# Inverse roots of a fused attention, local-attention and expert kernel: exp(-0.5 ln) on ScalarE in place of Sqrt, reciprocals and two of three Newton steps

## What is computed

```
def _layernorm(x, axis=-1, eps=1e-05):
    m = jnp.mean(x, axis=axis, keepdims=True)
    v = jnp.var(x, axis=axis, keepdims=True)
    return (x - m) / jnp.sqrt(v + eps)
...
    x = x + _L0_attn_ref(_layernorm(x, axis=-1), ...)
    x = x + _L0_ffn_ref(_layernorm(x, axis=-1), ...)
    x = x + _L1_attn_ref(_layernorm(x, axis=-1), ...)
    x = x + _L1_ffn_ref(_layernorm(x, axis=-1), ...)
```

```
        def l2norm(t):
            return t / jnp.maximum(jnp.linalg.norm(t, axis=-1, keepdims=True), 1e-12)
...
            xn = (x - mu) / jnp.sqrt(var + 1e-05) * g + bln
            hg = xn @ W1 + b1
            a, gate = jnp.split(hg, 2, -1)
            return a * jax.nn.gelu(gate, approximate=False) @ W2 + b2
```

## Time and profile before

| | us |
|---|---|
| median of 3 runs (lowest to highest) | 3120.57 (3115.48 to 3128.14) |
| the profiled execution's own time | 3113.61 |
| its span, first to last instruction | 3111.8 |
| PE busy | 2429.2 (78%) |
| DVE busy | 2169.8 (70%) |
| POOL busy | 1701.8 (55%) |
| ACT busy | 1605.2 (52%) |

### The profile page before, as it was taken

How to read it: one execution, slowest core, us unless ns; L and a number is a source line. 1 busy time by engine, 2 the same in 40 slices (tenths; PEclk the granted TensorE clock), 3 DMA queues, 4 the chain that set the end, 5 groups by cost and what they waited for, 6 DMA issues and landing times.

```text
span 3111.8 us, 59042 instructions
## 1 busy us (share of the span) xinstructions
PE 2429.2 (78%) x23892; PEld 1403.8 (45%) x23892; DVE 2169.8 (70%) x2127; ACT 1605.2 (52%) x1739; POOL 1701.8 (55%) x1799
## 2 busy tenths in 40 slices
PE   5777765888888988888889888888888757777253
PEld 1112124555555655556556565555565411122153
DVE  2654738988878888888888888888888336663301
ACT  2144554556666666666566666666666312456100
POOL 2222008877777777777777777777777140110202
PEclk5587988999999999999999999999999855999587
DMA  4111000000000000000000000000000010110122
GB/s 145 51 33 33 25 2 1 15 2 15 2 2 23 6 10 1 23 2 15 2 23 2 15 2 15 10 15 2 2 9 1 1 57 31 45 45 15 30 71 68
DMA packets 62506, 67.53 MB, mean 22 GB/s; under 512 B 13142, under 2 KB 51156, under 8 KB 62228
## 3 DMA queue, kind: packets, MB, share of 16 engines
q1 hardware_dynamic: 60100, 58.90, 6.2%
q0 software_dynamic: 2128, 4.72, 0.6%
HBM read 45.91 MB, written 17.56 MB: 20 GB/s over the span
## 4 chain that ended last, share of the span: by engine, by line
PE 39%; issue 19%; POOL 16%; DVE 16%; ACT 9%; POOLq 1%; DMA 1%; SPq 0%; DVEq 0%; ACTq 0%
PE bank L851 5%; DVE big L1414 5%; POOL small L577 4%; PE bank L933 4%; DVE big L1530 3%; PE bank L718 3%; PE bank L689 3%; PE bank L671 3%; POOL small L578 3%; ACT big L1170 2%; POOL big L588 2%; PE bank L894 2%; ACT pxs L1280 2%; PE bank L925 2%; PE bank L976 2%
## 5 line engine op out<-in xcount | busy, mean ns | idle before, releaser
L1414 DVE TENSOR_REDUCE big<-bank 128x1 f32<-128x512 f32 x512 | 325.9, 685 | 226.2 <-PE bank L689 219.3
L593 POOL TENSOR_TENSOR sc<-sc,small 128x1024 f32<-128x1024 f32 x96 | 263.5, 2745 | 332.6 <-DVE small L1551 332.6
L1530 DVE TENSOR_TENSOR big<-big,small 128x1024 f32<-128x1024 f32 x192 | 382.4, 1992 | 45.6 <-POOL small L580 45.6
L851 PE MATMUL bank<-wqk,xs 128*128 128x512 f32 x768 | 366.7, 623 | 20.9 <-ACT xs L1241 20.7
L933 PE MATMUL bank<-pxs,mw 128*128 128x256 f32 x1536 | 366.2, 382 | 0.0
L933 PEld LDWEIGHTS bank<-pxs,mw 128*128 128x128 f32 x1536 | 290.1, 192 | 99.5 <-issue 68.7
L1508 DVE TENSOR_REDUCE small<-big 128x32 f32<-128x2048 f32 x96 | 219.0, 2281 | 142.4 <-ACT big L1254 141.4
L1170 ACT ACTIVATE big<-bank 128x1024 f32<-128x1024 f32 x256 | 248.9, 1026 | 46.1 <-PE bank L703 45.5
L1267 ACT ACTIVATE sc<-bank 128x1024 f32<-128x1024 f32 x96 | 98.3, 1024 | 328.5 <-PE bank L903 328.5
L1280 ACT ACTIVATE pxs<-bank 128x1024 f32<-128x1024 f32 x192 | 186.3, 1022 | 143.5 <-PE bank L925 140.9
L577 POOL TENSOR_TENSOR small<-small 128x32 f32<-128x32 f32 x288 | 225.5, 783 | 36.9 <-DVE small L1510 21.9
(11 more groups left out here) (215 smaller groups left out, 4699.0 us busy)
## 6 DMA issues: line engine op xcount, KB each, us to landing
pxs<-part_rows SPq DMA_DIRECT2D x64, 224.0 KB
part_rows<-big SPq DMA_DIRECT2D x96, 128.0 KB
wqk<-in_L_ffn_w SPq DMA_DIRECT2D x32, 256.0 KB, 3.1
wqk<-in_L_ffn_Wqkv SPq DMA_DIRECT2D x12, 512.0 KB, 4.4
wvt<-in_wv_layers_t SPq DMA_DIRECT2D x6, 512.0 KB, 4.6
wol<-in_L_ffn_Wo SPq DMA_DIRECT2D x6, 512.0 KB, 7.1
w<-in_L_ffn_W SPq DMA_DIRECT2D x6, 341.0 KB
pxs<-big SPq DMA_DIRECT2D x96, 4.0 KB
```

The source lines that it names most:

```text
L593: pool.tensor_tensor(p3, p3, rden(i).unsqueeze(2).broadcast_to([P, LH, 64]), ALU.mult).then_inc(l_pn, 1)
L851: m = pe.matmul(bank[:, 2 - 2 * half + c, :], xs[:, b % 2, WIN + i * P:WIN + (i + 1) * P], wqk[:, (2 * half + c) * 512:(2 * half + c + 1) ...
L1414: dve.tensor_reduce(nm[:, qt, 2 * p + r:2 * p + r + 1], bank[:, 4 + r, :], AX.X, ALU.max, negate=True).then_inc(a_mx, 1)
L1530: dve.tensor_tensor(r3, r3, nrm(i)[:, half * LH:(half + 1) * LH].unsqueeze(2).broadcast_to([P, LH, LD]), ALU.mult).then_inc((l_yq, l_yk)[h ...
```

## The change

- In every layer norm ACT computes Ln of (variance + eps) and then Exp with scale -0.5, one waiting for the other, in place of Sqrt. DVE's reciprocal is gone, and DVE multiplies by ACT's result.
- For query and key norms DVE's integer guess is gone. ACT gets a new function `guess`: Ln and Exp on 128x32, behind the queries of each slot, waiting for DVE's sums of squares. POOL runs one Newton step where it ran three, and now waits for ACT instead of DVE.
- The table set that holds Ln and Exp is loaded at the start and behind every group of Gelus, by hand.

```
         def ln_scale(dve, k, dst):
             dve.wait_ge(ln_r, k + 1)
-            dve.reciprocal(sqn[:, :], rstd[:, :]).then_inc(ln_i, 1)
-            dve.wait_ge(ln_i, k + 1)
-            dve.tensor_tensor(dst, xc[:, :], sqn[:, :], ALU.mult).then_inc(ln_out, 1)
+            dve.tensor_tensor(dst, xc[:, :], rstd[:, :], ALU.mult).then_inc(ln_out, 1)
...
+        def ln_inverse_root(act, k, dst, src):
+
+            act.activation(dst, src, ACT.Ln, bias=eps[:, 0:1]).then_inc(ln_i, 1)
+            act.wait_ge(ln_i, k + 1)
+            act.activation(dst, dst, ACT.Exp, scale=-0.5).then_inc(ln_r, 1)
...
             for b in range(BATCH):
                 act.wait_ge(ln_var, base + b + 1)
-                act.activation(roots_all[:, b, :], bank[:, 4 + b, :], ACT.Sqrt, bias=eps[:, 0:1]).then_inc(ln_r, 1)
+                ln_inverse_root(act, base + b, roots_all[:, b, :], bank[:, 4 + b, :])
...
             def inverse_root(T, i):
-                pool.wait_ge(l_ss, T + 1)
+                pool.wait_ge(l_gs, T + 1)
                 settle(pool)
-                ch = Chain(pool, l_chn, T * 11)
+                ch = Chain(pool, l_chn, T * 3)
                 y, s, u = nrm(i), small[:, 0, :], small[:, 4, :]
-                for step in range(3):
-                    ch.link(pool.tensor_tensor(u, y, y, ALU.mult))
...
+                ch.link(pool.tensor_tensor(u, y, y, ALU.mult))
+                ch.link(pool.tensor_tensor(u, u, s, ALU.mult))
+                ch.link(pool.tensor_tensor(u, u, three_halves.broadcast_to([P, 2 * LH]), ALU.add))
+                pool.tensor_tensor(y, y, u, ALU.mult).then_inc(l_nr, 1)
...
+            def guess(T, i):
+
+                act.wait_ge(l_ss, T + 1)
+                settle(act)
+                act.activation(small[:, 4, :], small[:, 0, :], ACT.Ln, scale=-2.0).then_inc(l_ln, 1)
+                act.wait_ge(l_ln, T + 1)
+                settle(act)
+                act.activation(nrm(i), small[:, 4, :], ACT.Exp, scale=-0.5).then_inc(l_gs, 1)
...
                 keys(T, i)
                 queries(T, i)
+                if ahead >= 1:
+                    guess(T + 1, (i + 1) % 2)
                 if i == 3 and not first:
                     shift_ffn(it - 1, (b - 1) % BATCH)
                 if i == 1 and feeds:
                     gate(it - 2, 1)
                     gate(it - 2, 2)
+                    act.preload_act_table_set("natural_log_exp_and_others")
...
                 if i == 0 and feeds:
                     gate(it - 2, 0)
+                    act.preload_act_table_set("natural_log_exp_and_others")
...
                 ch.link(dve.tensor_reduce(ss, sq.rearrange("p (h d) -> p h d", d=LD), AX.X, ALU.add))
-                ch.link(dve.tensor_scalar(ss, ss, 1e-24, -0.5, ALU.max, ALU.mult))
-                dve.tensor_scalar(nrm(i).bitcast(I32), ss.bitcast(I32), -0.5, GUESS, ALU.mult, ALU.add).then_inc(l_ss, 1)
+                dve.tensor_scalar(ss, ss, 1e-24, -0.5, ALU.max, ALU.mult).then_inc(l_ss, 1)
```

More of the change, by code:

```diff
@@ L236, in build @@
             sem(n) for n in ("l_tab", "l_xs", "l_qk", "l_raw", "l_sq", "l_ss", "l_nr"))
-        l_chr, l_chn = sem("l_chr"), sem("l_chn")
+        l_chr, l_chn, l_ln, l_gs = sem("l_chr"), sem("l_chn"), sem("l_ln"), sem("l_gs")
         l_rb, l_ra, l_aq, l_ak, l_yq, l_yk = (sem(n) for n in ("l_rb", "l_ra", "l_aq", "l_ak", "l_yq", "l_yk"))
@@ L308, in ln_squares @@
             act.activation(sqn[:, :], xc[:, :], ACT.Square).then_inc(ln_sq, 1)
+        def ln_inverse_root(act, k, dst, src):
+            act.activation(dst, src, ACT.Ln, bias=eps[:, 0:1]).then_inc(ln_i, 1)
+            act.wait_ge(ln_i, k + 1)
+            act.activation(dst, dst, ACT.Exp, scale=-0.5).then_inc(ln_r, 1)
         def ln_root(act, k, b1):
             act.wait_ge(ln_var, k + 1)
-            act.activation(rstd[:, :], bank[:, b1, :], ACT.Sqrt, bias=eps[:, 0:1]).then_inc(ln_r, 1)
+            ln_inverse_root(act, k, rstd[:, :], bank[:, b1, :])
         def ln_scalar(act, k, b1):
@@ L370, in norm_all_vector @@
                 dve.wait_ge(ln_r, base + b + 1)
-                dve.reciprocal(roots_all[:, b, :], roots_all[:, b, :]).then_inc(ln_i, 1)
-                dve.wait_ge(ln_i, base + b + 1)
                 dve.tensor_tensor(zT[:, b, :], zT[:, b, :], roots_all[:, b, :], ALU.mult).then_inc(step_done, 1)
@@ L1296, in layer_root @@
                 act.wait_ge(ln_var, LAYER0 + j + 1)
-                act.activation(rstd_l, bank[:, 7, :], ACT.Sqrt, bias=eps[:, 0:1]).then_inc(ln_r, 1)
+                ln_inverse_root(act, LAYER0 + j, rstd_l, bank[:, 7, :])
             def gate(j, n):
@@ L1357, in _ @@
                 squares(T, T)
+            guess(0, 0)
             layer_slots(act, slot)
@@ L1496, in _ @@
             norm_all_vector(dve, SEED)
-            GUESS = float(0x5F3759DF - 0x40400000)
             ss, u_mx, u_den = small[:, 0, :], small[:, 1, 0:LH], small[:, 5, 0:LH]
             def square_sums(T, i):
-                ch = Chain(dve, l_chr, T * 2)
+                ch = Chain(dve, l_chr, T)
                 dve.wait_ge(l_sq, T + 1)
@@ L1578, in scale_norm @@
                 dve.wait_ge(ln_r, LAYER0 + j + 1)
-                dve.reciprocal(sqn[:, :], rstd_l).then_inc(ln_i, 1)
-                dve.wait_ge(ln_i, LAYER0 + j + 1)
-                dve.tensor_tensor(sqn[:, :], xc[:, :], sqn[:, :], ALU.mult).then_inc(ln_out, 1)
+                dve.tensor_tensor(sqn[:, :], xc[:, :], rstd_l, ALU.mult).then_inc(ln_out, 1)
                 dve.wait_ge(ln_out, LAYER0 + j + 1)
```

## The result

The changed kernel takes 3030.32 us (median of 4 runs, 3019.82 to 3036.36) where the kernel before takes 3121.15 beside it (4 runs): a ratio of 0.970, 95% interval 0.967 to 0.973, or 91 us less. The forecast was 57 us less (3063), and its range reached down to 3012. Compared a second time (experiment 10) the ratio is 0.974 (0.971 to 0.976), 78 us less.

A forecast was written before the change was run, and what follows sets the result against it. PE, 88% busy in the middle stage, waits on a chain through the Newton steps and one through ACT's Gelus; DVE bounds the first seven slots. Terms -15 + 7 - 22 - 13 - 10 - 4 = -57 us gave 3063 us, range 3012 to 3102.

The forecast's parts named there:

- What bounds the kernel: Middle stage: PE 88% busy; its waits end a Newton-step chain, which the change shortens, and an ACT chain, which it lengthens.
- Part 1: First seven slots, without feed-forward work: eight fewer POOL products and a faster query scaling save 2.2 us each, -15 us.
- Part 2: Other 22 sequences: gains of 3.6 us against losses on the Gelu chain, net +0.3 each, +7 us.
- Part 3, whole-batch norm: Whole-batch norm outside the slots: four reciprocals in a row go, gain 11.2 us, twice, -22 us.
- Norms that stand alone: Five norms, two per attention and the middle stage's last: Exp replaces the reciprocal, -2.6 us each, -13 us.
- Norms in the rounds: Four norms in the attentions' rounds: PE's 2.01 us wait goes and a load becomes an Exp, -10 us.
- the loads' -4: Table loads ahead of each attention's first exponentials and the expert router's: 3 x 1.28 us, -4 us.
- Guess waits for DVE: Slot i=1: ACT's `guess` waits for DVE's sums of squares, 95 us on top, some 3158 us; chance 0.05.
- Newton everywhere: All of 88 later slots: the Newton chain was the bound, each gains 2.2 us, 2862 us; chance 0.04.
- Plateau: Steady sequences: the Gelu chain wins, Part 2 at its upper end, 46 us above the sum, about 3108; chance 0.15.
- large gain: Steady sequences: the key turn's 1.36 us counts too and no clock is lost, -2.0 us each, 3012; chance 0.15.
- The drained switch: ACT's table loads: each holds ACT 2.66 us with a pause, 61 us above the sum, 3124 us; chance 0.03.

The follow-up runs named there:

- experiment 10: The changed kernel once more, unaltered, against the kernel before: 3031.06 us, ratio 0.9736.
- Experiment 4: The changed kernel with slot i=2's `guess` moved behind gates 1 and 2, so three Gelus share one table load: 2931.25 us, 0.9417 of the kernel before.
- experiment 6: The changed kernel with query and key norms as before, layer norms changed, and no load behind gate 0: 0.9653 of the kernel before.
- Experiment 5: The changed kernel with all three Newton steps on POOL again, the guess staying on ACT: 0.9807 of the kernel before.
- experiment 1: The changed kernel with Sqrt and DVE's reciprocal again in every layer norm outside the middle stage's slots: 0.9928 of the kernel before.
- experiment 2: The changed kernel with Sqrt and reciprocal again in only the four layer norms inside the attentions' rounds: 0.9798 of the kernel before.
- (3): The changed kernel with query and key norms as before, layer norms changed, both hand loads behind the gates kept: 0.9732 of the kernel before.

## Why the prediction came out as it did

- **What bounds the kernel.** Right. The two chains exchanged their waits (85 us went, 95 came). Experiment 4 confirms that the Gelu chain costs, and experiment 6 that with three Newton steps plain 1 takes over when it is relieved.
- **Part 1, -15.** Right mechanism, too small. The early sequences gave 19.7, eight intervals of 2.46 us where I had seven slots of 2.2, and the way from the whole-batch norm to the first softmax 3.0 more (38.87 to 35.87, one profile each). Experiment 5 gives all of the 19.7 to the eight products, and 2.1 of the 3.0. The scaling did not fall to 1.2 in all of these slots (it takes 1.24 to 2.02), but the slot no longer hangs on DVE, which now stands idle for 3.18 us in the one shown. That L1510 is worth nothing there is right too.
- **Part 2, +7.** Right in sum, as far as one profile of the kernel before can tell: four profiles with this middle stage (changed, its repeat, experiments 1 and 2) give 82.09, 82.78, 82.13 and 82.82, in the mean +0.4 per sequence, or +8. The terms were not right one by one. Step by step by the experiments: layer norms alone -1.8 (6), the two loads +1.2 (3), `guess` on ACT +1.4 (5), eight products -0.5 (changed). With a scatter of 0.5 to 0.7 between profiles the first three stand as to their sign and rough size; the last does not stand clear of nothing. I had given the layer norms 0.35: with DVE's reciprocal valued at nothing, PE's wait for DVE's normed input (6.2 us in 11 waits before, 620 to 2330 us) and part of that for the queries went as well, and plain 1's wait fell from 52.3 to 36.3. And I had given the products 3.25: once PE comes later for the Gelus, plain 1 has nothing left to wait for, with or without the eight products. The wait before gate 2 was 4.30 us where I had 4.5, and what PE lost to the clock behind it 1.5 where I had 0.7 to 1. Gains and losses in one chain don't add; what I subtracted as two sums was one maximum.
- **Part 3, whole-batch norm, -22.** From the first centring to the last product 21.9 and 23.3 us became 9.5 and 9.5. Of these 26.2 us 1.4 lie in the centrings of the second norm, ahead of the root, so 25 are the change's, 12.4 each where I had 11.2. ACT's pitch is 1.23 us per sequence, not 1.52, because Exp starts 0.03 us after Ln ends, where I had put a semaphore of 0.2, and the next Ln overlaps it.
- **Norms that stand alone, -13.** The four in the attentions wait 2.17 in place of 4.89, and the middle stage's last takes 6.3 us from centring to `xc` where it took 9.1: -2.7 each, right.
- **Norms in the rounds, -10: the term that was mis-sized.** From the start of the centring to the end of the product the four took 69.1 us and take 51.2: -4.5 each, 18 in all. It is not one profile's accident: 68.5 to 69.1 in the three profiles with the old norm there, 50.1 to 52.9 in the ten with the new. Two things were wrong. I took the one wait of 2.01 for all four; in the profile before they are 2.01, 3.36, 1.94 and 3.58, 10.9 us, and 0.4 is left of them. And I left out the clock, though I had counted it for plain 1: in experiment 2's trace the wait of 1.96 us follows a group of eight matmuls at a granted clock of 0.50 that runs at 1.00 with the new norm. That both come from Sqrt's reciprocal and second load is shown for the norm as a whole; how the clock's part divides between the two was not tried.
- **The sum.** With the measured terms (-23, +8, -25, -14, -18, and the loads' -4) it is -76. The comparisons gave -91 and -78, and experiment 1 gives the norms outside of the slots 60 to 71 where their terms here make 58 (25, 11 for the four alone in the attentions, 18, 4). What is left lies within the scatter that one profile has: the same middle stage took 1724 to 1739 us over its 21 sequences, the same first attention up to 10.6 us more or less. In the two profiles of the changed kernel the difference in the middle stage is PE's busy time (72.4 and 73.0 us per sequence for the same matmuls, at a granted clock of 0.960 and 0.953), while its idle time differs by 0.1. What sets the clock apart from run to run can't be said from these runs, and the loads' term was not tried by itself.
- **Rivals.** *Guess waits for DVE*: 0.6 us at most in the steady stretch, up to 2.0 in the early slots; it fell. *Newton everywhere*: the later slots gained nothing. *Plateau* and *large gain* of part 2: neither. *The drained switch*: in the rows above each load starts within 0.02 us of the end of what ran before it and the next activation 0.01 to 0.02 us after it ends, in the changed kernel as in experiment 4. The Trainium skill (ScalarE: Activation LUTs, What ACT_TABLE_LOAD costs) puts about 1380 ns of drain beside the load's 1283; the load's own length agrees with the 1.28 here, the drain does not show.

The range (3012 to 3102) held the time. The miss, 33 us at first and 21 at the repeat, is made of the rounds and the early slots (8 us each), the whole-batch norms (3) and scatter.

## What to carry over

Where two engines feed a third in the same stretch, price a change by which of the two then arrives last, not by adding what one saves to what the other loses: eight products were worth 2.5 us in a slot where their chain was last, and about 0.1, no more than the scatter, where it was not. When an activation function is swapped for one of another table set, look first at where the old set's groups stand: here the change as made broke one group of Gelus in two, and putting it together again gave as much (88 to 108 us) as the change itself. The order that takes most is the change with all Gelus of a sequence behind one load and with the copies that nobody awaits behind them: 2895 to 2899 us, 6.9% under the kernel before.

## What the runs showed of the hardware

- The printed granted clock can be wrong at the start of a profile: 1.00 over a matmul pair that took 1.97 us where it takes 1.07 at a recorded 1.00, in the three traces whose clock records begin only at 143 us. Check it against the duration of a known matmul.
- A long wait on PE can cost more than its length. Behind 4.30 us of waiting a pair of matmuls took 1.72 us for 1.09, and the scores 1.85 for 1.48; taking 3.2 us of idle time per sequence away gave 4.6. Behind waits of 0.84 and 1.57 us the pairs took 1.09 and 1.13, which is not longer.
- Dependent activations on ACT follow each other closely: 0.03 us from the end of Ln to the start of Exp on 128x512, 0.12 on 128x32.
- DVE's scaling, with both operands in SBUF, waits for the end of the key addition on POOL that it meets, and then runs at its own speed: 2.02 us for 0.94 of overlap and 1.16 of work. DVE's softmax difference, which reads PSUM, ran beside the same addition in 1.23 us, as without it.
